# Self attention: a select on GpSimd in place of the second causal mask on TensorE

## The chip, the cores and the metric

The kernel runs on one NeuronCore of a Trainium2 chip. The metric is the device time of one execution in microseconds (us). Matrix products run on TensorE (PE in the profile), reductions out of PSUM and norms on VectorE (DVE), exponentials and most copies out of PSUM on ScalarE (ACT), small elementwise work and gather or scatter DMAs on GpSimd (POOL).

## The reference, cut to what matters

Four blocks work on 32 batches of 112 rows with 256 columns: cross attention to a context, causal self attention, a mixture of eight experts, and a second cross attention with a quantised layer. The change lies in the second:

```
nx = layernorm(x, ln1_w, ln1_b)
q, k, v = split(nx @ Wqkv + bqkv, 3)             # 16 heads of 16
scores = einsum('bqhd,bkhd->bhqk', q, k) / sqrt(16)
scores = where(tril(ones), scores, finfo.min)    # a query sees no later key
attn = softmax(scores)
x = x + einsum('bhqk,bkhd->bqhd', attn, v).reshape(B, S, D) @ Wo + bo
```

A layernorm, the choice of two experts for each row, and the scatter of the rows to the experts' slots follow in the same loop.

## The kernel before, in words

`program` (L1734 on) calls four stages one after another: `cross_first`, `self_attention`, `experts`, `cross_last`. Each keeps one instruction stream per engine, and the streams meet only in semaphores. An engine works through its own stream in order: a wait holds back all that is written behind it. Those streams, written by hand, set the order of the work; nothing else plans it.

`self_attention` goes over the 32 batches with `over_batches`, whose function `step(b, par)` is called for b from -2 to 35. One step works on up to seven batches in different phases. For the batch b:

- TensorE, in this order within step b: `plain_scores` of b (four matmuls that write the mask `causal` at L1019, then 16 of q by k at L1028) into the four banks of `quad`; `values` of b-1 (16 matmuls at L1051, from `probsT` into `outs`); the expert logits and the rank of earlier batches (L1083, L258); q of b+1 (L1060); transposes of the attention's output of b-1 into rows (L1096); k of b+1 (L1060); transpose of the maxima of b (L1103); transposes of the normalised rows of b-1 (L1107); `scores` of b; transposes for b-2 (L1119); the output product of b-1 (L1125); v of b+1 (L1130); transposes of b+2 (L1137).
- `scores` writes the scores of b a second time into `quad`, transposed, with the keys on the partitions. The mask `causal_t` comes first (four matmuls of 448 columns, L1019), then the negated row maxima (16, L1036), then k by q (8, L1041). ScalarE takes exp of all 1792 columns into `probsT` (L864); `probsT` lies in a part of the tensor that the trace names `w`. Its sums come from a column of ones in `v`, inside `values`.
- VectorE in step b: statistics of b+2 (L231, L234), maxima of b out of `plain_scores` (L938), rank, reciprocal and product of b-1 (L951, L953), norm of b+2, norm of b-2, `place` and `choose` for older batches, norm of b+2 into `nn` (L245), then the output of b-1: L976, L979, its statistics, and v of b+1 (L986).
- GpSimd in step b: rstd of b+2 (L238, L240) and two instructions that keep it (L796, L797); q times the mask of heads (L801); rstd (L238, L240); two scatters of b-4 (L812); the residual of b-1 (L817), which waits for `o_added` from L979; rstd (L238, L240); a copy of b-2 (L824).

`held` instructions of one element (L810, L823) stand between a wait and the instruction that it is for. Two waits of TensorE's stream matter below: ahead of `plain_scores`, `wait(pe, exp_ready, b)`, since it overwrites `quad`; ahead of `values`,

```
pe.wait_ge(exp_ready, b)
pe.wait_ge(v_ready, b)
wait(pe, o_biased, b - 1)
values(1 - par)
```

Of the kernel before, what the change touches and what calls it, by code (L numbers as in the profile page):

```python
# [16 lines left out]
ALU = mybir.AluOpType  # L17
# [4 lines left out]
T = 112  # L22
# [18 lines left out]
def wait(eng, sem, value):  # L41

    if isinstance(value, int) and value <= 0:
        return
    eng.wait_ge(sem, value)


def exists(b, n=NB):

    return not isinstance(b, int) or 0 <= b < n  # L50


def over_batches(eng, step, before=1, after=1, first=2, last=2):


    for b in range(-before, first):
        step(b, b % 2)
    with eng.Fori(first // 2, (NB - last) // 2) as i:
        step(2 * i, 0)
        step(2 * i + 1, 1)  # L60
    for b in range(NB - last, NB + after):
        step(b, b % 2)
# [199 lines left out]
def row(ap, b):  # L262

    return ap[0:T, bass.ds(b, 1), :].rearrange("p a d -> p (a d)")
# [425 lines left out]
def self_attention(nc, mem, w, residual):  # L690
# [3 lines left out]
    with ExitStack() as ctx:  # L694
        sb = lambda n, shape, dt=F32: ctx.enter_context(nc.sbuf_tensor(f"s_{n}", shape, dt))
        sem = lambda n: ctx.enter_context(nc.semaphore(f"s_{n}"))
# [5 lines left out]
        ident_bf, causal, causal_t = (sb(n, [T, T], BF16) for n in ("ident_bf", "causal", "causal_t"))  # L702
        late = mem["w2"][:, NE - 1, :, :].rearrange("p c d -> p (c d)")
        probsT = late[0:T, 0:16 * T].rearrange("p (r c) -> p r c", r=4)
# [39 lines left out]
        scores_mm, exp_ready, values_mm = sem("scores_mm"), sem("exp_ready"), sem("values_mm")  # L744
        oT_ready, rows_mm, recip_ready, on_ready = sem("oT_ready"), sem("rows_mm"), sem("recip_ready"), sem("on_ready")
        oT2_mm, oT2_ready, op_mm, o_biased, o_added = sem("oT2_mm"), sem("oT2_ready"), sem("op_mm"), sem("o_biased"), sem("o_added")
        x_ready, stats_kept, n2_kept = sem("x_ready"), sem("stats_kept"), sem("n2_kept")
        n2T_mm, n2T_ready, gate_mm, gate_ready = sem("n2T_mm"), sem("n2T_ready"), sem("gate_mm"), sem("gate_ready")
        choose_step, chosen_ready, rank_mm, place_step, slot_ready = (sem(n) for n in ("choose_step", "chosen_ready", "rank_mm", "place_step", "slot_ready"))
# [18 lines left out]
        with nc.Block() as block:  # L768

            @block.sync  # L770
            def _(sp):
                sp.sem_clear(mem["spent"])
                for dst, src in loads:
                    sp.dma_start(dst, src).then_inc(weights_in, 16)
                for t in range(2):
                    for e in range(2):
                        for r in range(4):
                            at = (8 * t + 2 * r + e) * HD
                            sp.dma_start(wo[64 * e + HD * r:64 * e + HD * (r + 1), t, :], w["L0_ffn_Wo"][at:at + HD, :]).then_inc(wo_in, 16)
                sp.dma_start(mem["fc1_b"][:, :, :], w["L0_ffn_fc1_b"]).then_inc(mem["fc1_b_in"], 16)  # L780
                for e in range(NE - 1):
                    sp.dma_start(mem["w2"][:, e, :, :], w["fc2_t"][e].rearrange("(c p) d -> p c d", p=128)).then_inc(mem["w2_in"], 16)
                sp.wait_ge(values_mm, NB)
                sp.dma_start(mem["w2"][:, NE - 1, :, :], w["fc2_t"][NE - 1].rearrange("(c p) d -> p c d", p=128)).then_inc(mem["w2_in"], 16)

            @block.gpsimd
            def _(pool):
                pool.wait_ge(cleared, 1)
                pool.wait_ge(mem["slots_cleared"], 32 * (NB - 2))

                def step(b, par):
                    nxt, ahead = b + 1, b + 2
                    if exists(ahead):
                        norm_u.pool_rstd(pool, ahead)
                        pool.wait_ge(norm_u.rstd_ready, 2 * ahead + 2)
                        pool.tensor_copy(row(u_stats, ahead)[:, 0:1], norm_u.rstd[:, 1:2])  # L796
                        pool.tensor_tensor(row(u_stats, ahead)[:, 1:2], norm_u.moments[:, 0:1], norm_u.rstd[:, 1:2], ALU.mult)\  # L797
                            .then_inc(stats_kept, 1)
                    if exists(nxt):
                        pool.wait_ge(q_whole, nxt + 1)  # L800
                        pool.tensor_tensor(qT[1 - par][:, :, :, :], q[:, :, :].unsqueeze(2).to_broadcast([128, 2, 2, T]),  # L801
                                           mem["qmask"][:, :].unsqueeze(1).unsqueeze(3).to_broadcast([128, 2, 2, T]), ALU.mult)\
                            .then_inc(q_ready, 1)
                    if exists(ahead):
                        norm_n.pool_rstd(pool, ahead)
                    if exists(b - 4):
                        pool.wait_ge(slot_ready, b - 3)
                        pool.wait_ge(n2_kept, b - 3)

                        pool.tensor_tensor(held[:, 2 + par:3 + par], mem["minus_half"][0:1, :], mem["minus_half"][0:1, :], ALU.add)  # L810
                        for i in range(TOP):
                            pool.indirect_dma_start(mem["slots"], bass.IndirectOffsetOnAxis(ap=slot_now[par][i][:, :], axis=0),  # L812
                                                    n2_sent[par][:, :], None).then_inc(sent[par], 16)
                    if exists(b - 1):
                        pool.wait_ge(o_added, b)
                        x = row(residual, b - 1)
                        pool.tensor_tensor(x, x, y_rows[1 - par][:, :], ALU.add).then_inc(x_ready, 1)  # L817
                        norm_o.pool_rstd(pool, b - 1)
                    if exists(b - 2):
                        pool.wait_ge(norm_o.rows_ready, b - 1)  # L820
                        wait(pool, sent[par], 16 * (b - par - 2))

                        pool.tensor_tensor(held[:, par:par + 1], mem["minus_half"][0:1, :], mem["minus_half"][0:1, :], ALU.add)  # L823
                        pool.tensor_copy(n2_sent[par][:, :], n2[:, :]).then_inc(n2_kept, 1)  # L824

                over_batches(pool, step, 2, 4, 4)
                for i in range(2):
                    pool.wait_ge(sent[i], 16 * TOP * NB // 2)
# [180 lines left out]
            def _(pe):  # L1009
# [3 lines left out]
                def step(b, par):  # L1013
# [3 lines left out]
                    def masked(mask):  # L1017
                        for r in range(4):
                            pe.matmul(quad[0:T, r, 0:4 * T].rearrange("p (h t) -> p h t", h=4), ident_bf[:, :],  # L1019
                                      mask[:, :].unsqueeze(1).to_broadcast([T, 4, T]), start=True, stop=False, skip_group_check=True)  # L1020
# [9 lines left out]
                        last.then_inc(plain_mm, 1)  # L1030

                    def scores():
                        masked(causal_t)
                        for h in range(4):
                            for r in range(4):
                                pe.matmul(quad[0:T, r, h * T:(h + 1) * T], choice[group(r), h, :], shift[group(r), :],  # L1036
                                          start=False, stop=False, skip_group_check=True)
                        for t in range(2):
                            for r in range(4):
                                at = 2 * t * T  # L1040
                                last = pe.matmul(quad[0:T, r, at:at + 2 * T], kT[par][group(r), t, :],  # L1041
                                                 qT[par][group(r), t, :, :].rearrange("p e t -> p (e t)"),
                                                 start=False, stop=True, skip_group_check=True)
                        last.then_inc(scores_mm, 1)
# [28 lines left out]
                        wait(pe, exp_ready, b)  # L1073
                        plain_scores()
                    if exists(b - 1):
                        pe.wait_ge(exp_ready, b)
                        pe.wait_ge(v_ready, b)
                        wait(pe, o_biased, b - 1)
                        values(1 - par)
# [29 lines left out]
                    if exists(b):  # L1109
                        pe.wait_ge(shift_ready, b + 1)  # L1110
                        scores()
# [20 lines left out]
                    if exists(ahead):  # L1132
# [5 lines left out]
                        last.then_inc(nT_mm, 1)  # L1138

                over_batches(pe, step, 2, 4, 4)  # L1140
                pe.wait_ge(slot_ready, NB)
                pe.matmul(rank_out, ones[:, :], earlier[:, :], start=True, stop=True).then_inc(total_mm, 1)
# [660 lines left out]
```

## Time and profile before

| what | value |
|---|---|
| median of 3 runs | 2145.3 us (2142.04 to 2145.58) |
| the profiled execution, its own time | 2148.3 us |
| its span, first to last instruction | 2146.3 us |
| TensorE busy | 1999.6 us (93%) |
| VectorE busy | 1390.0 us (65%) |
| ScalarE busy | 1022.8 us (48%) |
| GpSimd busy | 889.4 us (41%) |
| mean granted TensorE clock | 0.971 of full speed |

The self attention takes the stretch from about 537 to 902 us of the span. The busy share of the whole says little of one stage, so what is read is one step of its loop, engine by engine. A time in front of a row is its start from the beginning of the span; "idle before" is how long the engine had nothing to do, and `<-` names what ended it.

### The profile page before, as it was taken

The numbers are of one execution on the slowest core, as the hardware profiler recorded it, in microseconds if no ns is written. First come the engines' busy times: TensorE is split into PE (matmuls) and PEld (weight loads), VectorE is DVE, ScalarE is ACT, GpSimd is POOL, SyncE is SP. The second block draws the span as 40 slices with busy tenths as digits, with TensorE's granted clock in tenths as the row PEclk, the third lists the DMA queues.
The fourth block names the chain that finished last, engine by engine and source line by source line (L and its number), as shares of the span: only waits on it lengthen the run. The fifth ranks groups of instructions, "written<-read, shape, count | busy, mean of one in ns | idle before, by whom it ended". The sixth has DMA issues, their size and how long they took to land. (4 is left out here: it accounts for less than half of the span.)

```text
span 2146.3 us, 61038 instructions
## 1 busy us (share of the span) xinstructions
PE 1999.6 (93%) x21235; PEld 1659.7 (77%) x21236; DVE 1390.0 (65%) x3586; ACT 1022.8 (48%) x2370; POOL 889.4 (41%) x1479
## 2 busy tenths in 40 slices
PE   5999999996899999589999999779999999999996
PEld 4888888885677777479999999657777777777774
DVE  5777777773688888543333333247887878788875
ACT  2555555553444444223223232246666666666662
POOL 4454554541466666400000000145656666665651
PEclk9999999998999999799999999979999999999998
DMA  7223323251400000111111111210111111011100
GB/s 209 90 85 103 95 92 105 82 210 29 143 22 21 21 21 21 51 57 37 34 39 34 37 37 34 87 34 22 37 31 36 31 29 39 27 39 29 36 20 9
DMA packets 98810, 118.87 MB, mean 55 GB/s; under 512 B 9794, under 2 KB 91458, under 8 KB 98626
## 3 DMA queue, kind: packets, MB, share of 16 engines
q1 hardware_dynamic: 92610, 103.43, 15.8%
q0 software_dynamic: 6144, 14.69, 2.3%
q8 instruction: 36, 0.59, 0.1%
q14 instruction: 20, 0.16, 0.0%
HBM read 67.36 MB, written 50.72 MB: 55 GB/s over the span
## 5 line engine op out<-in xcount | busy, mean ns | idle before, releaser
L1245 ACT ACTIVATE e_act_T<-ps_quad,fc_b 128x128 f32<-128x128 f32 x504 | 136.8, 383 | 313.3 <-PE ps_quad L1310 313.3
L1310 PEld LDWEIGHTS ps_quad<-e_xT,e_w_now 128*128 128x128 f32 x2016 | 236.4, 193 | 7.9 <-DVE e_xT L1279 4.1
L1310 PE MATMUL ps_quad<-e_xT,e_w_now 128*128 128x128 f32 x2016 | 237.4, 276 | 3.5 <-DVE e_xT L1279 3.5
L1325 PE MATMUL ps_out<-w,e_act_T 128*128 x1008 | 228.1, 379 | 0.8 <-DVE e_y L1287 0.8
L1423 POOL COPY c_index<-slot 112x1 uint32 (+1 forms) x64 | 19.4, 332 | 477.7 <-POOLq L1208 477.7
L419 ACT ACTIVATE a_probsT<-ps_quad 125x1792 f32<-125x1792 f32 x96 | 159.9, 1665 | 100.6 <-PE ps_quad L579 100.6
L1276 DVE COPY e_w_now<-w 128x2048 f32 x63 | 77.3, 1227 | 200.2 <-PE ps_quad L1310 190.3
L1325 PEld LDWEIGHTS ps_out<-w,e_act_T 128*128 128x128 f32 x1008 | 186.6, 190 | 24.0 <-issue 1.2
L1450 POOL TENSOR_TENSOR c_kL<-c_kT,c_kH 128x376 fp32r<-128x376 f32 x128 | 126.3, 986 | 172.0 <-ACT c_kH L1502 171.4
L206 ACT ACTIVATE c_probs<-ps_quad,c_negmax 112x375 f32<-112x375 f32 x256 | 144.0, 571 | 29.7 <-DVE c_negmax L167 29.7
L1497 ACT ACTIVATE c_kT<-ps_proj 128x376 f32<-128x376 f32 x128 | 61.9, 484 | 182.8 <-PE ps_proj L258 181.4
L167 DVE TENSOR_REDUCE c_negmax<-ps_quad 112x2 f32<-112x750 f32 x128 | 120.0, 937 | 43.4 <-PE ps_quad L136 35.2
L178 DVE TENSOR_SCALAR c_probs<-c_probs,c_recip 112x375 f32<-112x375 f32 x256 | 144.0, 603 | 4.6
L476 DVE TENSOR_REDUCE a_negmax<-ps_turned 112x2 f32<-112x750 f32 x128 | 120.2, 939 | 33.8 <-PE ps_turned L565 33.7
L474 DVE TENSOR_REDUCE a_negmax<-ps_quad 112x4 f32<-112x1500 f32 x64 | 110.2, 1722 | 36.6 <-PE ps_quad L565 36.6
L258 PE MATMUL ps_proj<-c_cH,c_wkH 128*128 128x376 f32 x256 | 100.3, 392 | 32.3 <-DVE c_wvH L1564 20.8
L147 PE MATMUL ps_turned<-ident,c_probs 112*125 112x112 f32 x768 | 107.9, 277 | 1.6 <-DVE c_probs L178 1.4
L147 PEld LDWEIGHTS ps_turned<-ident,c_probs 112*125 112x125 f32 x768 | 96.3, 189 | 10.4 <-issue 10.0
L1287 DVE TENSOR_TENSOR e_y<-ps_out,e_b 128x256 f32<-128x256 f32 x63 | 26.7, 424 | 119.0 <-PE ps_out L1325 119.0
L158 PE MATMUL ps_out<-c_probsT,c_v 125*64 125x112 f32 x1536 | 101.9, 268 | 0.2 <-ACT c_probsT L199 0.2
L158 PEld LDWEIGHTS ps_out<-c_probsT,c_v 125*64 125x64 f32 x1536 | 74.5, 136 | 34.6 <-issue 30.5
L199 ACT ACTIVATE c_probsT<-ps_turned 125x672 f32<-125x672 f32 x128 | 93.8, 733 | 4.7 <-PE ps_turned L147 4.7
(308 smaller groups left out, 5331.6 us busy)
## 6 DMA issues: line engine op xcount, KB each, us to landing
slots<-a_zeros SPq DMA_DIRECT2D x60, 512.0 KB, 4.9
a_cT<-in_ctx_t SPq DMA_DIRECT2D x32, 375.0 KB, 3.6
c_cT<-in_ctx_t SPq DMA_DIRECT2D x32, 375.0 KB, 3.2
w<-in_fc_t SPq DMA_DIRECT2D x2, 4096.0 KB, 20.1
w<-in_fc_t SPq DMA_DIRECT2D x8, 1024.0 KB, 11.7
e_xg<-slots SPq DMA_DIRECT2D x63, 128.0 KB, 2.0
slots<-e_y SPq DMA_DIRECT2D x63, 128.0 KB, 1.7
out<-c_fo SPq DMA_DIRECT2D x32, 112.0 KB, 1.9
```

What stands on the lines that cost most here:

```text
L147: last = pe.transpose(self.turned[u % sets][:, j, c * T:(c + 1) * T], self.probs[u % 4][:, j, c * self.chunk:(c + 1) * self.chunk], ident[ ...
L158: last = pe.matmul(self.out[row:row + self.vdim, block * T:(block + 1) * T], v(u, j, c), self.probsT[u % 2][:, j, c, :], start=(c == 0), s ...
L167: dve.tensor_reduce(self.negmax[:, u % 4, :], self.scores[u % len(self.scores)], AX, ALU.max, negate=True).then_inc(self.max_ready, 1)
L178: last = dve.tensor_scalar(p, p, self.recip[:, u % 4, j:j + 1], None, ALU.mult)
L206: last = act.activation(self.probs[u % 4][:, j, :], self.scores[u % len(self.scores)][:, j, :], ACT.Exp, bias=self.negmax[:, u % 4, j:j + ...
L419: act.activation(probsT[:, 2 * i:2 * i + 2, :, :].rearrange("p c r x -> p r c x"), quad[0:KC, :, 0:2 * HALF].rearrange("p r (c x) -> p r c ...
L474: dve.tensor_reduce(rows[:, :, 0], quad[0:T, :, 0:CTX], AX, ALU.max, negate=True).then_inc(max_ready, 1)
L476: dve.tensor_reduce(rows[:, 2 * half:2 * half + 2, 0], plain[0:T, :, 0:CTX], AX, ALU.max, negate=True)\
L1245: last = act.activation(act_T[par][:, c * TILE:(c + 1) * TILE], hidden[par][:, c // 4, (c % 4) * TILE:(c % 4 + 1) * TILE], ACT.Gelu, bias= ...
L1310: last = pe.matmul(hidden[par][:, c // 4, (c % 4) * TILE:(c % 4 + 1) * TILE], w1_now[:, k, c * 128:(c + 1) * 128], xT[par][:, k, :], start ...
L1325: last = pe.matmul(y_ps[:, 0:D], act_T[1 - par][:, c * TILE:(c + 1) * TILE], w2[:, bass.ds(e, 1), c, :].rearrange("p a d -> p (a d)"), sta ...
L1450: pool.tensor_tensor(kL[to][:, tile, :], kT[:, tile, :], kH[to][:, tile, :], ALU.subtract).then_inc(k_ready, 1)
```

## The change

GpSimd gets a new piece in step b, behind its first norm and ahead of the product with the mask of heads. It waits until the exponentials of batch b-1 are there, and sets to zero, in place, all those of `probsT` whose key (partition) is later than its query (column). TensorE writes no `causal_t` into `quad`; the first matmul of each group now starts the sum. `values` waits for `causal_ready` from GpSimd in place of `exp_ready`. The mask of `plain_scores` stays, so the row maxima are still taken over the allowed keys alone.

```diff
+        causal_ready, mask_held = sem("causal_ready"), sb("mask_held", [1, 1])
...
                         pool.tensor_tensor(row(u_stats, ahead)[:, 1:2], norm_u.moments[:, 0:1], norm_u.rstd[:, 1:2], ALU.mult)\
                             .then_inc(stats_kept, 1)
+                    if exists(b - 1):
+                        pool.wait_ge(exp_ready, b)
+                        pool.tensor_tensor(mask_held[:, :], mem["minus_half"][0:1, :], mem["minus_half"][0:1, :], ALU.add)
+                        pool.affine_select(probsT, probsT, [[0, 4], [0, 4], [1, T]], ALU.is_ge, 0.0, base=0, channel_multiplier=-1).then_inc(causal_ready, 1)
                     if exists(nxt):
                         pool.wait_ge(q_whole, nxt + 1)
...
                     def scores():
-                        masked(causal_t)
                         for h in range(4):
                             for r in range(4):
                                 pe.matmul(quad[0:T, r, h * T:(h + 1) * T], choice[group(r), h, :], shift[group(r), :],
-                                          start=False, stop=False, skip_group_check=True)
+                                          start=True, stop=False, skip_group_check=True)
...
                     if exists(b - 1):
-                        pe.wait_ge(exp_ready, b)
+                        pe.wait_ge(causal_ready, b)
                         pe.wait_ge(v_ready, b)
                         wait(pe, o_biased, b - 1)
                         values(1 - par)
```

How the instructions of GpSimd follow one another in the loop's step, before (a row names the output, then the inputs; ISA and REGISTER_ALU are waits and counters):

```order
L796 COPY s_u_stats<-s_norm_u_rstd 112x1
L797 ISA
L797 TENSOR_TENSOR s_u_stats<-s_norm_u_moments,s_norm_u_rstd 112x1
L801 TENSOR_TENSOR s_qT<-s_q,qmask 128x448
L238 TENSOR_TENSOR s_norm_n_rstd<-s_norm_n_moments,eps 112x1
```

And after:

```order
L797 COPY s_u_stats<-s_norm_u_rstd 112x1
L798 ISA
L798 TENSOR_TENSOR s_u_stats<-s_norm_u_moments,s_norm_u_rstd 112x1
L802 TENSOR_TENSOR s_mask_held<-minus_half 1x1
L803 AFFINE_SELECT w<-w 112x1792
L806 TENSOR_TENSOR s_qT<-s_q,qmask 128x448
L238 TENSOR_TENSOR s_norm_n_rstd<-s_norm_n_moments,eps 112x1
```

The select stands last behind everything that GpSimd does for the step before and behind the rstd of b+2; the product for q of b+1 stands behind it.

TensorE in the loop's step, before, from the transposes of b-1 to the `values` of the next step:

```order
L1107 MATMUL ps_out<-ident,s_on 128x112 x2
L1019 MATMUL ps_quad<-s_causal_t,s_ident_bf 112x448 x4
L1036 MATMUL ps_quad<-s_shift,s_choice 112x112 x16
L1041 MATMUL ps_quad<-s_qT,s_kT 112x224 x8
L1119 MATMUL ps_turned<-ident,s_n 128x112 x2
L1125 MATMUL ps_out<-s_wo,s_oT 112x256 x2
L1130 MATMUL ps_turned<-s_wqkv,s_nT 112x256 x2
```

And after:

```order
L1111 MATMUL ps_out<-ident,s_on 128x112 x2
L1040 MATMUL ps_quad<-s_shift,s_choice 112x112 x16
L1045 MATMUL ps_quad<-s_qT,s_kT 112x224 x8
L1123 MATMUL ps_turned<-ident,s_n 128x112 x2
L1129 MATMUL ps_out<-s_wo,s_oT 112x256 x2
L1134 MATMUL ps_turned<-s_wqkv,s_nT 112x256 x2
```

Four mask matmuls are gone; all else keeps its place, `values` included.

## Rows read from the trace of the kernel before

**Rows 1.** Page, busy times; then PE, PEld, DVE, ACT, POOL, clock, steady stretch.

```profile
PE 1999.6 (93%) x21235; PEld 1659.7 (77%) x21236; DVE 1390.0 (65%) x3586; ACT 1022.8 (48%) x2370; POOL 889.4 (41%) x1479
...
600.00:860.00 260.00, 257.01 (x3566) 205.35 (x3566) 219.45 (x908) 126.94 (x295) 168.02 (x374) 1.00 0.07 22
```

**Rows 2.** Timeline of TensorE, one step: start us, us, what, [idle before].

```profile
620.19 1.05 PE L1028 MATMUL ps_quad<-s_kT,s_qT 32*112 32x112 f32 x32
621.17 0.97 PE L1051 MATMUL ps_out<-w,s_v 112*32 112x112 f32 x32
...
623.56 0.60 PE L1096 MATMUL ps_out<-ident,s_oT 128*112 128x128 f32 x4
...
624.97 0.41 PE L1107 MATMUL ps_out<-ident,s_on 112*128 112x112 f32 x2
625.49 0.96 PE L1019 MATMUL ps_quad<-s_causal_t,s_ident_bf 112*112 112x448 bf16 x4
...
627.97 1.03 PE L1125 MATMUL ps_out<-s_wo,s_oT 128*112 128x256 f32 x4
...
629.70 0.36 PE L1137 MATMUL ps_proj<-ident,s_nn 112*128 112x112 f32 x2
...
631.73 0.97 PE L1051 MATMUL ps_out<-w,s_v 112*32 112x112 f32 x32
```

**Rows 3.** Timelines: two exponentials on ScalarE, the matmul after the first.

```profile
554.73 1.66 ACT L864 ACTIVATE w<-ps_quad 112x1792 f32<-112x1792 f32 x1 [1.95 <-PE ps_quad L1041]
...
556.53 0.94 PE L1019 MATMUL ps_quad<-s_causal,s_ident_bf 112*112 112x448 bf16 x4 [0.65 <-ACT w L864]
...
627.87 1.67 ACT L864 ACTIVATE w<-ps_quad 112x1792 f32<-112x1792 f32 x1 [1.70 <-PE ps_quad L1041]
```

**Rows 4.** Timeline of VectorE in the same step.

```profile
624.20 0.26 DVE L951 RECIPROCAL s_recip<-ps_out 112x16 f32<-112x16 f32 x1 [0.61 <-PE ps_out L1096]
...
628.72 0.41 DVE L245 TENSOR_SCALAR s_nn<-s_u_rows,s_norm_n_moments,s_norm_n_rstd 112x256 f32<-112x256 f32 x1
629.16 0.48 DVE L976 SCALAR_TENSOR_TENSOR s_o<-ps_out,s_u_stats,s_bo 112x256 f32<-112x256 f32 x1
```

**Rows 5.** Timeline of GpSimd in the same step and the one before.

```profile
623.27 0.19 POOL L797 TENSOR_TENSOR s_u_stats<-s_norm_u_moments,s_norm_u_rstd 112x1 f32 x1
...
630.52 0.72 POOL L817 TENSOR_TENSOR residual<-residual,s_y_rows 112x256 f32 x1 [0.42 <-issue]
...
632.01 0.18 POOL L823 TENSOR_TENSOR s_held<-minus_half 1x1 f32<-1x1 f32 x1
632.14 0.39 POOL L824 COPY s_n_sent<-s_n 112x256 f32<-112x256 f32 x1
...
633.63 0.19 POOL L797 TENSOR_TENSOR s_u_stats<-s_norm_u_moments,s_norm_u_rstd 112x1 f32 x1
```

**Rows 6.** Groups of GpSimd instructions: count, busy us, mean ns, idle before.

```profile
L377 POOL TENSOR_TENSOR a_cL<-a_cT,a_cH 128x376 fp32r<-128x376 f32 x64 | 62.2, 993 | 2.6
...
L801 POOL TENSOR_TENSOR s_qT<-s_q,qmask 128x448 f32<-128x448 f32 x32 | 29.8, 932 | 41.3 <-ACT s_q L845 41.3
L371 POOL CAST a_cH<-a_cT 128x376 fp32r<-128x376 f32 x64 | 29.8, 489 | 0.0
```

**Rows 7.** Stretches of 2 us, columns as in rows 1, around idle TensorE.

```profile
882.00:884.00 2.00, 0.60 (x3) 0.18 (x1) 0.82 (x2) 0.96 (x1) 0.55 (x1) 1.00 0.29 90
920.00:922.00 2.00, 2.00 (x13) 2.00 (x13) 0.00 (x0) 0.00 (x0) 0.00 (x0) 0.58 0.11 36
...
1436.00:1438.00 2.00, 1.48 (x9) 1.20 (x10) 0.62 (x1) 0.00 (x0) 2.00 (x3) 0.77 0.00 0
```

**Rows 8.** Timeline of TensorE, other stretches: an idle time and two speeds.

```profile
889.02 2.02 PE L1125 MATMUL ps_out<-s_wo,s_oT 128*112 128x256 f32 x4 [0.17 <-ACT s_oT L860]
...
918.01 5.57 PE L1310 MATMUL ps_quad<-e_xT,e_w_now 128*128 128x128 f32 x32 [0.82 <-DVE e_xT L1279]
...
1436.52 0.43 PE L136 MATMUL ps_quad<-c_kH,c_qH 64*112 64x376 f32 x2 [1.78 <-issue]
```

## The prediction

> **What bounds the kernel now.** I read the page first: TensorE is busy for 1999.6 us, 93% of the span [rows 1]. Then the stretch from 600 to 860 us, in the middle of the self attention: TensorE is busy for 257.0 of 260 us at full clock, VectorE for 219, GpSimd for 168 [rows 1]. So TensorE sets the pace there, and a first reading says that four matmuls less per batch are a pure gain. A gain on a full engine only counts if nothing new is put into its path, so the timeline of one step comes next. The `values` matmuls start at 621.17 and those of the next step at 631.73, so a step takes about 10.55 us [rows 2], and no row of TensorE between them shows an idle time.
>
> The question is where the new wait of `values` ends. The exponentials are not the issue: they run from 627.87 to 629.54 [rows 3], two microseconds ahead of `values` at 631.73. The select however stands in GpSimd's stream behind L797, and L797 of the step whose `values` start at 621.17 begins at 623.27 and ends at 623.46 [rows 5]. GpSimd comes to the select 2.3 us after TensorE wants its result. That is the core of the case: the wait is late by GpSimd's place in line, before the select has cost anything.
>
> **A ring that closes.** A late wait would be paid once if GpSimd did not depend on it. It does. I follow the ring from one `values` to the next, each piece from the start of one row to the start of the next:
>
> - `values` 621.17 to VectorE's reciprocal at 624.20: 3.03 us, in which TensorE does `values`, logits, rank, q and the transposes L1096 (end 624.16) [rows 2, 4].
> - reciprocal 624.20 to L976 at 629.16: 4.96 us. L976 needs the output product L1125 (627.97, end 629.00) [rows 2], but VectorE itself ends `nn` (L245) at 629.13 [rows 4]. VectorE's own queue sets this piece.
> - L976 to GpSimd's residual L817 at 630.52: 1.36 us [rows 4, 5].
> - L817 to the end of L797 at 633.63 + 0.19 = 633.82: 3.30 us of GpSimd's stream in one piece [rows 5].
>
> Sum: 12.65 us, against a step of 10.55. Today nobody waits for that end, so it costs nothing. Behind the change `values` waits for it.
>
> **The change part by part.**
>
> - Removed, four mask matmuls per batch: the `causal_t` block at 625.49 takes 0.96 us [rows 2]; its last matmul runs beside the next block, so I count 0.9 us of TensorE per step, 29 us for 32 batches. In the ring it saves nothing: L1125 would end at 628.1 in place of 629.00, and L976 still waits for VectorE at 629.13. I take 0; the ends are 0 and 0.1.
> - Added, one `mask_held`: as L823 to L824, 632.01 to 632.14, it moves the stream by 0.13 us [rows 5].
> - Added, the wait from GpSimd to TensorE: the nearest row is exp to mask, end 556.39, start 556.53 [rows 3]: 0.14 us.
> - Added, the select itself, 112 partitions by 1792 elements. The trace has no such instruction. From below: one input, 376 elements in 489 ns [rows 6]; with 0.19 us for an instruction of one element (L797) [rows 5] that is 0.80 ns for each further element, so 0.19 us + 1791 x 0.80 ns = 1.62 us. From above: two inputs, 376 elements in 993 ns, 2.14 ns each, 4.02 us. The product of L801, with two inputs of which one is repeated, takes 932 ns for 448 [rows 6], or 1.66 ns each: 3.2 us. The select reads one input but must make up a second value and compare, so it lies between the copy and L801. I take 2.8 us and keep 1.62 and 4.02.
>
> The Trainium skill, GPSIMD Engine Reference, section "Performance pitfalls for Q7 kernels", gives bodies that compare and select 2.03 cycles for an element, or 1.03 when unrolled by two, at the 1.2 GHz of its section "Specifications". As an estimate that is 3.0 or 1.5 us here, and the step would be 0.2 us longer or 1.3 us shorter than mine; no row of this trace shows a select.
>
> Step with TensorE at full clock: 12.65 + 0.13 + 2.8 + 0.14 = 15.72 us, that is 5.17 longer.
>
> - The clock. In that step TensorE has work up to the end of `plain_scores`. They end at 621.2 today, 10.55 us behind the `values` before. Without the masks they could end 0.9 sooner, but L1137 waits for `nn` (629.13 against 629.70 today [rows 2, 4]), so the saving is 0.5 and they end 10.1 us behind `values`. Until 15.7 TensorE stands still, 5.6 us in each step. What a gap can do is in the trace: an idle time of only 1.78 us ahead of 1436.52 lies in a stretch whose mean clock fell to 0.77 [rows 7, 8], so it dropped to the lower level in it. Against it stands 882 to 884, with TensorE busy for 0.60 of 2 us and the clock at 1.00 [rows 7]. With 5.6 us I expect the drop to 1.2 GHz in nearly each step. It ends only after TensorE has worked again for a while: the matmuls that began at 918.01 behind an idle time were still slow for most of 920 to 922, mean 0.58 [rows 7, 8], so some 3.7 us. At the low clock a block takes twice as long: L1125 2.02 us at 889.02, against 1.03 [rows 2, 8]. The first piece of the ring, 2.99 us of TensorE work, is what falls into that. With 3.7 us slow it grows by 1.85, if slow throughout by 2.99. I take 2.4. The piece from reciprocal to L976 stays VectorE's as long as the clock is back by then.
>
> A step: 15.72 + 2.4 = 18.1 us, 7.57 longer. There are 32 `values`, so 31 intervals: 235 us. The first and last steps have less of GpSimd's work and more of other waits, which I leave at zero. The profiled execution took 2148.3 us, so 2383; the median of the runs lies 3 below it: **2380 us**.
>
> **What is late next, and who queues.** Behind the select on GpSimd stands L801, the product for q of the next batch. It needs a product that TensorE starts only behind `values`, and idles 41.3 us in 32 times for it today [rows 6], so it loses nothing. The scatters follow and the residual, which already waits for L979. `plain_scores` of the next batch and VectorE's maxima run while TensorE waits for the select.
>
> **The rivals.**
>
> 1. *The ring, but the clock holds.* For it: 882 to 884. Against it: 1436 [rows 7]. Then 31 x 5.17 = 160 us more: 2305. With a select of 1.62 or 4.02 us it is 2268 or 2343. Chance 0.20.
> 2. *The clock stays low past the transposes.* Then the first piece grows by 2.99, and TensorE's work from L1107 at 624.97 to the end of L1125 at 629.00 [rows 2], 4.0 - 0.9 = 3.1 us without the masks, takes 6.3 against the 4.2 in which VectorE gets to L976 and adds 2.1. A step is 15.72 + 2.99 + 2.1 = 20.8 us, 10.3 longer: 2145 + 318 = 2463. For it: TensorE has short waits in that piece too, which could keep the clock down. Against it: work without a pause had the clock back after 3.7 us at 918. Chance 0.10.
> 3. *Faster: the select is hidden.* If GpSimd reached the select early enough, behind the exponentials' end at 629.54 and done by 631.73, the 29 us come in whole: 2116. It would need GpSimd to be through with L797 by 631.73 - 2.8 - 0.3 = 628.6, and today that is 633.82. L817 alone, which waits for `o_added`, keeps it beyond that. The point from which it decides is the select's start against `values`; the rows have it 5 us on the wrong side. Chance 0.02.
> 4. *The change does not take its price*: the select costs so little or the ring bends so that the step stays at 10.6 us. Nothing in the rows supports it. Chance 0.01.
>
> The forecast has 0.67. Its own range, by the select's ends (-37 and +38 us) and the clock's (-17 and +18), is 2326 to 2436. The range from 2280 to 2450 takes in most of rival 1 and leaves out most of rival 2. A measurement of this kernel tells 0.2%, some 4 us, from no change. Only rival 3 is faster, only rival 4 is the same, all the rest is slower by far.
>
> **What would show it.** In the profile after: GpSimd's select starts right behind `mask_held`, with a mean time between 1.62 and 4.02 us; TensorE has 32 idle times ahead of the `values` matmuls, ended by the select, some 5 us each; between two starts of `values` lie 17 to 19 us; VectorE's piece from reciprocal to L976 is still near 5 us; the granted clock in the middle of the stage is well under 1.00, about 0.8, and `values` at the head of each step take about twice 0.97 us. The other three stages keep their times. It is wrong if the stage's TensorE rows show no idle time there, or if the step is longer than 20 us with a select under 4.

## The result, and the profile after

| what | before | after |
|---|---|---|
| median, measured side by side | 2144.97 us (4 runs) | 2334.69 us (4 runs, 2332.72 to 2337.71) |
| the profiled execution, its own time | 2148.3 us | 2337.7 us |
| its span | 2146.3 us | 2335.9 us |
| mean granted TensorE clock | 0.971 | 0.918 |

The ratio of the medians is 1.0889 (the 95% interval is 1.087 to 1.0908), so the change costs 190 us. The forecast was 2380, its range 2280 to 2450. In the profile after, the lines of the self attention have moved by four or five: the select is L803, `values` L1055, the reciprocal L956, L976 is now L981, L979 is L984, L1125 is L1129, L817 is L822.

The page's busy times after:

```profile
PE 2072.1 (89%) x21107; PEld 1739.8 (74%) x21108; DVE 1388.6 (59%) x3586; ACT 1022.9 (44%) x2370; POOL 951.0 (41%) x1543
```

The same stretch of 600 to 860 us as in [rows 1], with the columns told there:

```profile
600.00:860.00 260.00, 195.47 (x2143) 167.12 (x2135) 132.75 (x559) 77.31 (x180) 133.96 (x264) 0.75 0.04 13
```

TensorE has 128 matmul records less than before, and yet it is busy for 72 us more. In the stretch it is busy for 195 us where it was 257, at a mean clock of 0.75 where it was 1.00. Fewer matmuls, more busy time and a lower clock belong together: each matmul at the low clock is counted for longer. Every engine has idle time in the stretch, so no engine bounds it. That is what a ring of waits looks like.

The group of the select after (busy us, mean ns, idle before):

```profile
L803 POOL TENSOR_SCALAR_AFFINE_SELECT w<-w 112x1792 f32<-112x1792 f32 x32 | 57.4, 1793 | 0.0
```

And the view of waits in the stage (us in total, times, longest):

```profile
PE ps_out L1055 <- POOL w L803: 124.7, 32, 5.1
```

The select takes 1.79 us, not the 2.8 of the prediction. All 32 `values` wait for it, 3.9 us each. Now the timeline of TensorE over one step after, to be laid beside [rows 2]:

```profile
655.99 1.72 PE L1055 MATMUL ps_out<-w,s_v 112*32 112x112 f32 x32 [4.17 <-POOL w L803]
...
660.42 1.06 PE L1100 MATMUL ps_out<-ident,s_oT 128*112 128x128 f32 x4
...
665.35 1.03 PE L1129 MATMUL ps_out<-s_wo,s_oT 128*112 128x256 f32 x4
...
668.12 1.05 PE L1033 MATMUL ps_quad<-s_kT,s_qT 32*112 32x112 f32 x32
673.22 0.97 PE L1055 MATMUL ps_out<-w,s_v 112*32 112x112 f32 x32 [4.04 <-POOL w L803]
```

The same step on VectorE and GpSimd, to be laid beside [rows 4, 5]:

```profile
661.51 0.26 DVE L956 RECIPROCAL s_recip<-ps_out 112x16 f32<-112x16 f32 x1 [2.43 <-PE ps_out L1100]
...
666.54 0.48 DVE L981 SCALAR_TENSOR_TENSOR s_o<-ps_out,s_u_stats,s_bo 112x256 f32<-112x256 f32 x1 [0.37 <-PE ps_out L1129]
...
667.89 0.72 POOL L822 TENSOR_TENSOR residual<-residual,s_y_rows 112x256 f32 x1 [0.75 <-DVE s_y_rows L984]
671.00 0.19 POOL L798 TENSOR_TENSOR s_u_stats<-s_norm_u_moments,s_norm_u_rstd 112x1 f32 x1
671.15 0.18 POOL L802 TENSOR_TENSOR s_mask_held<-minus_half 1x1 f32<-1x1 f32 x1
671.29 1.79 POOL L803 TENSOR_SCALAR_AFFINE_SELECT w<-w 112x1792 f32<-112x1792 f32 x1
```

The ring can be walked in these rows from 655.99 to 673.22: `values` to reciprocal 5.52 us (predicted 3.03 plus 2.4 of clock), reciprocal to L981 5.03 (4.96), L981 to the residual 1.35 (1.36), the residual to the end of L798 3.30 (3.30), `mask_held` and select to `values` 2.03. In the step after it the same ring loses its time elsewhere:

```profile
678.00 0.26 DVE L956 RECIPROCAL s_recip<-ps_out 112x16 f32<-112x16 f32 x1 [2.50 <-PE ps_out L1100]
...
683.49 0.48 DVE L981 SCALAR_TENSOR_TENSOR s_o<-ps_out,s_u_stats,s_bo 112x256 f32<-112x256 f32 x1 [0.81 <-PE ps_out L1129]
...
690.10 1.72 PE L1055 MATMUL ps_out<-w,s_v 112*32 112x112 f32 x32 [4.17 <-POOL w L803]
```

Here `values` to reciprocal is 4.78 us, and reciprocal to L981 5.49, because VectorE waits 0.81 us for the output product. Steps of 17.25 us, like the first, and of 16.88, like the second, follow one another, 17.07 on average. The first three and the last three of the 31 are shorter: 12.1, 15.4, 16.2, and 15.9, 12.0, 14.6.

The clock in slices of 1 us (the column behind the five engines):

```profile
653.00:654.00 1.00, 0.00 (x0) 0.00 (x0) 1.00 (x1) 0.00 (x0) 0.84 (x3) 0.81 0.00 0
654.00:655.00 1.00, 0.00 (x0) 0.00 (x0) 0.02 (x1) 0.00 (x0) 1.00 (x3) 0.50 0.00 0
...
663.00:664.00 1.00, 1.00 (x12) 0.67 (x14) 0.85 (x6) 0.62 (x3) 0.60 (x2) 0.57 0.00 0
664.00:665.00 1.00, 1.00 (x32) 0.78 (x28) 0.68 (x8) 0.38 (x2) 0.47 (x3) 1.00 0.00 0
...
674.00:675.00 1.00, 1.00 (x14) 0.88 (x6) 0.00 (x0) 0.54 (x1) 0.00 (x0) 0.55 0.00 0
```

The clock falls from 2.4 to 1.2 GHz in the idle time and comes back near 663.9, after 7.9 us of work without a pause. In the next step `values` still run at full clock (673.22, 0.97 us); the clock falls 0.9 us after they began, and the matmuls behind them are slow all the same. The idle time had ended by then. The low clock of this step lasts from 674.1 to about 680.9, 6.8 us. A slow stretch need not start inside the gap ahead of it. The trace of before shows the same behind the idle time that ended at 1436.52 [rows 8]: in slices of 1 us the clock is 1.00 up to 1437 and 0.55 in the next.

The signs that the prediction named came in the main: 32 idle times ended by the select, a select between 1.62 and 4.02 us, steps of 17.07 us in the middle, at the lower end of 17 to 19, and a clock of 0.75 there. The idle times are 3.9 us where some 5 were expected, and `values` take twice 0.97 us in every second step only.

### The profile page after: what moved, and what is told of

It is laid out like the page before. It is cut to its first block and busy times, and to the rows that moved or that the text cites. A ratio compares the mean times of both kernels' runs of the same rounds, so it can differ in the third digit from the quotient of the medians.

```text
span 2335.9 us, 60849 instructions
## 1 busy us (share of the span) xinstructions
PE 2072.1 (89%) x21107; PEld 1739.8 (74%) x21108; DVE 1388.6 (59%) x3586; ACT 1022.9 (44%) x2370; POOL 951.0 (41%) x1543
## 3 DMA queue, kind: packets, MB, share of 16 engines
q1 hardware_dynamic: 92610, 103.43, 14.4%
## 5 line engine op out<-in xcount | busy, mean ns | idle before, releaser
L1055 PE MATMUL ps_out<-w,s_v 112*32 112x112 f32 x1024 | 43.6, 330 | 124.7 <-POOL w L803 124.7
L178 DVE TENSOR_SCALAR c_probs<-c_probs,c_recip 112x375 f32<-112x375 f32 x256 | 148.9, 622 | 4.6
L1055 PEld LDWEIGHTS ps_out<-w,s_v 112*32 112x32 f32 x1024 | 33.1, 139 | 130.9 <-POOL w L803 76.4
L845 ACT ACTIVATE s_oT<-ps_out 128x448 f32<-128x448 f32 x32 | 17.4, 544 | 200.6 <-PE ps_out L1055 200.6
```

Source lines behind the costliest of these rows:

```text
L178: last = dve.tensor_scalar(p, p, self.recip[:, u % 4, j:j + 1], None, ALU.mult)
```

## The experiments

Ten kernels ran. Each edit is shown against the kernel after; a "step" is the distance between the starts of two `values`. Each ratio is to the kernel before, measured beside it: 2149.63 us for the first four, 2150.89 for the sixteen products and for the select behind the residual, 2148.68 for the other four. The kernel after was measured once, beside 2144.97, so its difference to these ten is good to some 6 us.

**The wait alone.** Is it the select's duration or GpSimd's place in line that costs?

```diff
-pool.tensor_tensor(mask_held[:, :], ..., ALU.add)
-pool.affine_select(probsT, ...).then_inc(causal_ready, 1)
+pool.tensor_tensor(mask_held[:, :], ..., ALU.add).then_inc(causal_ready, 1)
...
 def scores():
+    masked(causal_t)
```

> The select is left out and the causal_t mask of TensorE is back, so the arithmetic is that of the kernel before; what stays of the change is the place of the wait: values waits for the one-element instruction on GpSimd behind L797. Ring theory: the step is 12.65 + 0.13 + 0.14 = 12.9 us with the clock held, 31 x 2.4 us more than before, so 2145 + 73 = 2218 us; if the shorter idle time of TensorE (some 2.3 us a step) still costs clock, up to 1.85 us a step more, 2276 us. Rival, the select's own time is the cost and the place is harmless: 2145 us, within 5.

Measured: 2268.67 us, ratio 1.0552 (1.0533 to 1.057). With no select, and with TensorE's mask as before, the wait costs 119 us. Two starts of `values` from TensorE's timeline:

```profile
654.87 0.97 PE L1055 MATMUL ps_out<-w,s_v 112*32 112x112 f32 x32 [2.08 <-POOL s_mask_held L802]
...
667.91 1.56 PE L1055 MATMUL ps_out<-w,s_v 112*32 112x112 f32 x32 [2.41 <-POOL s_mask_held L802]
```

That step is 13.04 us long, near the ring's 12.65 plus one small instruction. Others take up to 16.8, and the mean is 14.4: an idle time of some 2 us is already followed by the low clock in many steps (mean 0.89 between 600 and 860 us). So the place in line costs before any select has run; the view that the price is the select's alone, and this kernel as fast as the one before, falls.

**The mask left out.** What are the four matmuls worth by themselves? The select is out, `values` waits for `exp_ready`, and TensorE writes no `causal_t`, so this kernel doesn't mask later keys in the exponentials.

```diff
-if exists(b - 1): ... pool.affine_select(probsT, ...)
...
-pe.wait_ge(causal_ready, b)
+pe.wait_ge(exp_ready, b)
```

> The causal_t mask is left out and nothing put in its place (later keys are not masked in the exponentials); values waits for exp_ready as before. Theory: outside the ring the four matmuls are worth their 0.9 us a step, 29 us in all: 2116 us; if VectorE or GpSimd bound the shorter step first, 2120 to 2130. Rival, the masks are hidden beside other work anyway: 2145 us.

Measured: 2132.42 us, ratio 0.9923 (0.99 to 0.9946), 17 us less. That is over half of the 29 us that TensorE's rows promise. The stretch from 600 to 860 us shows both engines, TensorE at 248 of 260 us where it was 257, and VectorE at 221 where it was 219 [rows 1]:

```profile
600.00:860.00 260.00, 248.20 (x3535) 196.56 (x3534) 221.28 (x927) 133.13 (x303) 170.51 (x372) 1.00 0.07 23
```

TensorE's timeline says why no more is won:

```profile
653.72 0.41 PE L1137 MATMUL ps_proj<-ident,s_nn 112*128 112x112 f32 x2 [0.33 <-DVE s_nn L245]
```

TensorE now waits for `nn` in each of the 25 steps between 600 and 860 us, 7.0 us in all: VectorE is next in line. The prediction had it so and let 0.5 of the 0.9 us through; in the middle it is 0.22, steps of 10.33 us for 10.55. The shorter steps at both ends give the rest, and a first `values` that comes 3.3 us sooner. So the most that this change could have brought with VectorE's stream as it is, is some 17 us.

**The select ahead of the residual**, in the same step as its exponentials.

```diff
-if exists(b - 1): pool.wait_ge(exp_ready, b) ...            # behind L798
+if exists(b): pool.wait_ge(exp_ready, b + 1) ...            # behind the scatters
```

> The same select, moved in GpSimd's stream from behind L797 of the next step to ahead of the residual (L817 of the kernel before), behind the two scatters. Ring theory: it starts when the scatters end, 8.9 us behind values, and ends at 10.8, so the step is about 11.0 us: 2150 to 2180 us. Rival, GpSimd's extra 1.8 us a step is what costs, wherever it stands: it stays near 2335 us.

Measured: 2174.23 us, ratio 1.0116 (1.0097 to 1.0135). The same instructions, put elsewhere in GpSimd's stream, cost 25 us in place of 190. The clock in the middle stays at 1.00 and the steps are 11.6 us long. Part of what is left has a cause that I had not expected. The group of L984 on VectorE:

```profile
L984 DVE SCALAR_TENSOR_TENSOR s_y_rows<-residual,s_u_stats,s_o 112x256 f32<-112x256 f32 x32 | 74.3, 2321 | 4.9 <-DVE s_o L981 4.7
```

And one of its rows in the timeline beside the select on GpSimd:

```profile
643.08 2.60 DVE L984 SCALAR_TENSOR_TENSOR s_y_rows<-residual,s_u_stats,s_o 112x256 f32<-112x256 f32 x1 [0.18 <-DVE s_o L981]
...
643.60 1.79 POOL L818 TENSOR_SCALAR_AFFINE_SELECT w<-w 112x1792 f32<-112x1792 f32 x1
```

L984 took 0.485 us before and takes 2.32 us now. It ends at 645.68, just behind the select's end at 645.39. That adds 1.8 us per step to VectorE, the engine that is next in line. The next reciprocal starts 3.8 or 4.1 us behind `values`, where it was 3.0. The step is 0.6 us longer than the ring's 11.0; how much of the 25 us is this hold and how much the ring, is not measured apart.

**The select ahead of the scatters**, earlier still.

```diff
-if exists(b - 1): pool.wait_ge(exp_ready, b) ...            # behind L798
+if exists(b): pool.wait_ge(exp_ready, b + 1) ...            # ahead of the scatters
```

> The same select, moved further up, ahead of the two scatters. It can start when the exponentials are there, 7.4 us behind values, and ends at 9.4, ahead of the 9.7 us that TensorE needs for a step without the masks. Ring theory: 9.7 to 10.6 us a step, 2118 to 2147 us; GpSimd then has some 9.7 us of work and gaps per step and may bound it itself. Rival, GpSimd's extra time is what costs wherever it stands: near 2335 us.

Measured: 2219.17 us, ratio 1.0325 (1.0306 to 1.0344): a clear miss. Between 600 and 860 us no wait of `values` for the select is left. The group of `nn` on VectorE:

```profile
L245 DVE TENSOR_SCALAR s_nn<-s_u_rows,s_norm_n_moments,s_norm_n_rstd 112x256 f32<-112x256 f32 x32 | 45.9, 1434 | 7.2 <-POOL s_norm_n_rstd L240 7.2
```

And a row of TensorE's timeline that waits for it:

```profile
714.49 0.41 PE L1141 MATMUL ps_proj<-ident,s_nn 112*128 112x112 f32 x2 [1.89 <-DVE s_nn L245]
```

Here the select stands beside `nn`, which takes 1.43 us in place of 0.41, up to 2.1. TensorE waits 1.9 us for it, and the clock falls in many steps (mean 0.89 between 600 and 860 us, steps of 12.6 to 13.8 us). In the four of the 20 steps in which `nn` runs free, another is held: L984 twice, and twice L913, a product of 112x16 (1.81 us in place of 0.17). The wait was gone and the contention had taken its place. How the 70 us divide between the hold and the clock is not measured.

**The gap filled, too long.** If the low clock is a cost of its own, matmuls without use in the gap should give it back.

```diff
+wait(pe, o_biased, b - 1)
+for i in range(30):
+    pe.matmul(outs[:, 0:128], ident[:, :], ident[:, :], ...)
 pe.wait_ge(causal_ready, b)
 pe.wait_ge(v_ready, b)
-wait(pe, o_biased, b - 1)
```

> The changed kernel with 30 more matmuls of TensorE (identity by identity, 128 columns, into the bank that values overwrites) behind plain_scores and ahead of the wait for the select. They compute nothing that is used; they fill some 3.5 of the 4.2 us in which TensorE stands idle. Clock theory: of the 6 us that a step is longer, 4.2 are the ring with the clock held and 1.85 the lower clock behind the gap; with the gap filled the granted clock stays near 1.00, the step is 12.65 + 0.13 + 1.79 + 0.14 = 14.7 us and the kernel takes about 2145 + 129 = 2275 us. Rival, the clock is only a symptom and the ring does not run over TensorE's slow part: 2335 us or more.

Measured: 2354.99 us, ratio 1.0955 (1.0937 to 1.0973). The filling was sized wrongly. Thirty such products took twice the time that I had given them, and themselves held `values` back by 2.9 us behind the select's end at 644.04:

```profile
640.06 6.96 PE L1082 MATMUL ps_out<-ident 128*128 128x128 f32 x60
646.95 0.97 PE L1055 MATMUL ps_out<-w,s_v 112*32 112x112 f32 x32
```

The clock did stay at 1.00, but the time said nothing. So it was repeated with about half as many.

**The gap filled, short enough.** The same edit with `range(16)`.

> The kernel after, with 16 matmuls of the identity with itself (128 columns) ahead of the wait of `values` for the select; their result in `outs` is overwritten by `values`. Thirty of them took 6.96 us, 0.23 us each, so 16 take 3.7 us, and the gap that they fill, from the end of `plain_scores` (10.1 us behind `values`) to the select's end (14.6), is 4.5 us at full clock: they end before the select. Theory (the ring is 12.65 + 0.13 + 1.79 + some 0.1 = 14.7 us, and the rest of what the change costs is the lower clock of the steps' beginnings): step 14.7 us, clock near 1.00, in all 2149 + 31 x 4.15 = 2278 us, 57 us faster than the kernel after. Rival (the rest is not the clock but other waits of the ring, which an idle TensorE does not cause): no gain, 2335 us, with steps of 16.5 us at whatever clock.

Measured: 2268.50 us, ratio 1.055 (1.0533 to 1.0568). Sixteen useless products per batch make the kernel after 66 us faster. The middle of the stage:

```profile
600.00:860.00 260.00, 244.54 (x3099) 204.63 (x3101) 159.04 (x663) 94.75 (x216) 155.27 (x300) 1.00 0.05 16
```

TensorE, VectorE and GpSimd in one step:

```profile
645.99 0.97 PE L1055 MATMUL ps_out<-w,s_v 112*32 112x112 f32 x32 [0.58 <-POOL w L803]
...
656.42 3.84 PE L1082 MATMUL ps_out<-ident 128*128 128x128 f32 x32
660.47 0.97 PE L1055 MATMUL ps_out<-w,s_v 112*32 112x112 f32 x32 [0.21 <-POOL w L803]
...
649.01 0.26 DVE L956 RECIPROCAL s_recip<-ps_out 112x16 f32<-112x16 f32 x1 [1.11 <-PE ps_out L1102]
...
653.87 0.48 DVE L981 SCALAR_TENSOR_TENSOR s_o<-ps_out,s_u_stats,s_bo 112x256 f32<-112x256 f32 x1
...
655.22 0.72 POOL L822 TENSOR_TENSOR residual<-residual,s_y_rows 112x256 f32 x1 [0.29 <-issue]
...
658.49 0.18 POOL L802 TENSOR_TENSOR s_mask_held<-minus_half 1x1 f32<-1x1 f32 x1
```

This is the ring at full clock: 3.02, 4.86, 1.35 and 3.27 us up to `mask_held`, then 0.14, 1.79 and 0.05 to `values` at 660.47, 14.48 in all. Steps of 14.49 and 14.63 alternate, 14.56 on average. The steady steps of the kernel after are 17.07, so the clock costs 2.51 us in each. In the first of the two steps shown for the kernel after it lies in the first piece, 5.52 against 3.02. In the second, 1.76 lie there (4.78) and 0.5 or 0.6 in the piece to L981 (5.49 against 4.86 here and 4.99 in the steps between), which waits for a late output product. Here L981 does not wait for it.

**The mask back on TensorE**, with the select kept. The prediction gave the removed matmuls nothing.

```diff
 def scores():
+    masked(causal_t)
```

> The changed kernel with the causal_t mask of TensorE written again, beside the select. The prediction has the removed mask at nothing, since VectorE's own queue holds L976: 2335 us. The profile after shows L981 (L976 before) waiting 0.74 us a step for the output product, because TensorE was slow ahead of it, so part of the 0.9 us should come back: 2335 + 20 to 28 = 2355 to 2363 us.

Measured: 2366.45 us, ratio 1.1013 (1.0995 to 1.1032), 32 us above the kernel after. Within the profiled executions the mean step goes from 16.56 to 17.33 us, 24 us in all, so I put it at 24 to 32. Some steps take 17.1 us, as without the masks, others up to 18.7. VectorE's row shows where a late step loses:

```profile
652.82 0.48 DVE L981 SCALAR_TENSOR_TENSOR s_o<-ps_out,s_u_stats,s_bo 112x256 f32<-112x256 f32 x1 [1.84 <-PE ps_out L1130]
```

In the kernel after L981 waited 0.4 or 0.8 us for the output product; in the late steps here it waits 1.5 to 1.9, so the masks push that product back by about a microsecond, and it is in the ring.

**The select twice** on the same data, the second behind its own wait and `mask_held`.

```diff
-pool.affine_select(probsT, ...).then_inc(causal_ready, 1)
+pool.affine_select(probsT, ...).then_inc(first_done, 1)
+pool.wait_ge(first_done, b)
+pool.tensor_tensor(mask_held[:, :], ..., ALU.add)
+pool.affine_select(probsT, ...).then_inc(causal_ready, 1)
```

> The changed kernel with the select executed twice, one behind the other with a semaphore and a one-element instruction between. Ring theory: every microsecond of GpSimd ahead of causal_ready is a microsecond of each of 31 steps, so 1.79 + 0.15 to 0.3 us each, 60 to 65 us: 2395 to 2400 us; if the longer idle time of TensorE costs more clock, up to 1.1 us a step on top, 2434 us. Rival, the select's time is partly hidden: under 2365 us.

Measured: 2442.40 us, ratio 1.1366 (1.1347 to 1.1385), 108 us more, or 3.5 per step. The two selects start 2.02 us apart:

```profile
647.92 1.79 POOL L804 TENSOR_SCALAR_AFFINE_SELECT w<-w 112x1792 f32<-112x1792 f32 x1
...
649.94 1.79 POOL L807 TENSOR_SCALAR_AFFINE_SELECT w<-w 112x1792 f32<-112x1792 f32 x1
651.87 1.72 PE L1059 MATMUL ps_out<-w,s_v 112*32 112x112 f32 x32 [6.04 <-POOL w L807]
```

So 2.0 us of the 3.5 is the ring, one for one, and the rest came with more time at the low clock (mean of the span 0.904 against 0.918). Its greater part stands in the piece from the reciprocal to L985 (L981 of the kernel after), which takes 5.7 and 7.0 us in turn in most of the middle, where it took 5.03 and 5.49:

```profile
724.52 0.48 DVE L985 SCALAR_TENSOR_TENSOR s_o<-ps_out,s_u_stats,s_bo 112x256 f32<-112x256 f32 x1 [2.44 <-PE ps_out L1133]
```

The first piece is 5.52 us in every step now. This is what rival 2 of the prediction describes, the clock low past the transposes. The time lies 8 us above the highest that was expected of the run.

**The select in quarters**, at the place ahead of the residual: if a VectorE instruction is held only until the running GpSimd instruction ends, four short ones should hold it less.

```diff
+for r in range(4):
+    part = pool.affine_select(probsT[:, r, :], ..., [[0, 4], [1, T]], ...)
+part.then_inc(causal_ready, 1)
```

> The select ahead of the residual as in the run before_residual, cut into four selects of 448 columns. There VectorE's L984, with both inputs in SBUF, took 2.3 us in place of 0.48 beside the select. Port theory: it waits until the instruction running on GpSimd ends, so with quarters of some 0.5 us L984 takes at most 1.0 us, VectorE gains 1.3 us a step and the kernel takes 2150 to 2165 us, against 2174. Rival, it waits for the whole piece of GpSimd work or for something else: L984 stays at 2.3 us and the time at 2174 or a little over.

Measured: 2184.32 us, ratio 1.0158 (1.0141 to 1.0175), 10 us slower than the single select at that place. The two groups, and the rows of two steps:

```profile
L986 DVE SCALAR_TENSOR_TENSOR s_y_rows<-residual,s_u_stats,s_o 112x256 f32<-112x256 f32 x32 | 29.0, 907 | 4.9 <-DVE s_o L983 4.0 <-issue 0.7
...
L819 POOL TENSOR_SCALAR_AFFINE_SELECT w<-w 112x448 f32<-112x448 f32 x128 | 70.1, 574 | 0.0
...
634.14 2.18 POOL L819 TENSOR_SCALAR_AFFINE_SELECT w<-w 112x448 f32<-112x448 f32 x4
634.46 2.14 DVE L986 SCALAR_TENSOR_TENSOR s_y_rows<-residual,s_u_stats,s_o 112x256 f32<-112x256 f32 x1 [0.18 <-issue]
...
645.82 0.67 DVE L986 SCALAR_TENSOR_TENSOR s_y_rows<-residual,s_u_stats,s_o 112x256 f32<-112x256 f32 x1 [0.18 <-DVE s_o L983]
646.20 0.34 POOL L817 TENSOR_TENSOR s_mask_held<-minus_half 1x1 f32<-1x1 f32 x1
646.50 2.18 POOL L819 TENSOR_SCALAR_AFFINE_SELECT w<-w 112x448 f32<-112x448 f32 x4
```

VectorE's instruction falls from 2.32 to 0.91 us on average, but not as the theory had it. In most steps, as at 645.82, L986 now goes first: GpSimd's `mask_held` takes 0.34 us in place of 0.18, and the quarters start when L986 has ended. Six times in the profiled execution L986 started as the first quarter began or ran. Five times, as at 634.46, it took 2.14 to 2.48 us and ended 0.28 us behind the last quarter, so it was not let in between them; once it was, behind the first (0.59 us). That speaks for the rival, the whole piece of GpSimd's work, and against a hold that ends with the instruction. Why L986 comes first here in steps in which it did not beside the single select, the runs do not show.

The time is a miss too. Four selects take 2.18 us from first start to last end against 1.79, L986 pushes them back where it goes first, `values` wait 34.4 us for them in total where they waited 19.7, and the clock falls in some steps: those of 11.58 us, much as before, are mixed with others of 12.0 to 12.6.

**The select behind the residual**, a place that the ring prices by itself, and where VectorE reads PSUM beside it.

```diff
 pool.tensor_tensor(x, x, y_rows[1 - par][:, :], ALU.add).then_inc(x_ready, 1)
+if exists(b): pool.wait_ge(exp_ready, b + 1) ... pool.affine_select(...)
 norm_o.pool_rstd(pool, b - 1)
```

> The select of batch b stands in step b right behind the residual of b-1 and ahead of the norm that follows it. Theory (the ring alone sets it): `values` to the residual 3.03 + 4.96 + 1.36 = 9.35 us, the residual 0.72, one small instruction 0.13, the select 1.79, to TensorE 0.1: a step of 12.1 us, 1.55 longer than before, 2149 + 48 = 2197 us with the clock held. The idle time that TensorE then has ahead of `values` is some 2.0 us; in the run with the wait alone about as much cost 1.5 us per step through the clock, and with that it is 2243. Rival (what costs is only the contention of the select with VectorE's instructions, which here stands at another place, beside the copy of the last q, k or v and the statistics): under 2180 us.

Measured: 2212.93 us, ratio 1.0267 (1.0227 to 1.0306), with single runs from 2198 to 2228. From its timelines:

```profile
647.35 0.72 POOL L818 TENSOR_TENSOR residual<-residual,s_y_rows 112x256 f32 x1 [0.34 <-issue]
648.04 0.18 POOL L821 TENSOR_TENSOR s_mask_held<-minus_half 1x1 f32<-1x1 f32 x1
648.06 0.42 DVE L231 BATCH_NORM_STATS2 s_norm_u_stats<-residual 112x6 f32 x1
648.18 1.79 POOL L822 TENSOR_SCALAR_AFFINE_SELECT w<-w 112x1792 f32<-112x1792 f32 x1
...
648.62 2.00 DVE L944 TENSOR_REDUCE s_negmax<-ps_quad 112x16 f32<-112x1792 f32 x1
...
650.03 1.17 PE L1056 MATMUL ps_out<-w,s_v 112*32 112x112 f32 x32 [1.77 <-POOL w L822]
```

Steps at full clock take 12.04 us; the ring gave 12.1. Others take 13.4 to 15.4, with the clock low in part of them. The mean clock of the four runs, 0.951 to 0.965, goes with their times, the lowest with the longest. The rival (contention alone, under 2180) falls: L985 is back at 485 ns, and the maxima L944, read from PSUM beside the select, take their 2.0 us as ever. So do the statistics L231, which read the residual in SBUF, with 0.42 us.

None of the four placements of the select beats the kernel before. Only the kernel without the mask does, and it leaves out part of the computation.

## Why the prediction was right, and where its sizes were off

- **The ring** (12.65 us at full clock) held. With the clock held it measures 12.50 us up to `mask_held`, and each piece agrees within 0.1. The other placement was priced from the same rows at 12.1 and came out at 12.04. Moving the select takes away up to 165 of the 190 us, and the wait alone, without a select, costs 119, so the place in GpSimd's stream decides.
- **The select** was priced at 2.8 us between 1.62 and 4.02, and takes 1.79. This term failed most: 1.01 us x 31 = 31 us too much. I argued that a compare must lie above a copy. The group of the select [after, above] puts its elements at (1.79 - 0.19) / 1791 = 0.89 ns, near the 0.80 of the copy in [rows 6] and far from the 1.66 and 2.14 of the products. That fits a price by the number of inputs read, but these are four kinds of work and no run varied the inputs alone. The estimate from the Trainium skill, GPSIMD Engine Reference, section "Performance pitfalls for Q7 kernels", was 3.0 or 1.5 us; the trace sides with the faster of its two figures, and with neither exactly.
- **The joints.** With a select of 1.79 my terms give 14.71 us at full clock, and 14.56 are measured: `mask_held` began before L798 had ended, and the handover to TensorE took 0.05 or 0.06 us where I had 0.14. That is 0.15 us x 31 = 4.7 us.
- **The clock** at 2.4 us per step measures 2.51, and that agreement is partly luck. I had slow work last 3.7 us, from the stretch at 918 to 922 [rows 7, 8]; here it lasts 7.9 and 6.8 us in turn. I had all of the cost in the first piece, which grows by 2.5 us in one kind of step and by 1.76 in the other, 2.13 on average. The rest is the start of rival 2: L981 waits 0.4 or 0.8 us for the output product (23.8 us in 32 steps), and its piece takes 5.03 or 5.49 us against 4.86 or 4.99 with the gap filled. "VectorE's own queue sets this piece" therefore holds at full clock and fails in the kernel after: there L981 waits for TensorE's output product in every step between 600 and 860 us.
- **The removed masks** were priced at 0. At full clock that is nearly so: L981 has no wait for the output product with the gap filled, and its piece takes 4.86 or 4.99 us without the masks, 4.96 with them in the kernel before and 5.16 with them in the wait alone (a step of 13.04 us). In the slowed ring they are worth 24 to 32 us, as the run with the mask back shows. The zero did not spoil the sum, since I put nothing on that piece for the clock either, and without the masks it stays at 5.03 and 5.49 us; the sentence that they save nothing in the ring was wrong.
- **The first and last steps** I left at the length of the others. Over the first three and last three, the kernel after is 16 us short of 6 x 17.07, the kernel before 1.5 short of 6 x 10.55. That is 14.6 us.

Together these give 31 + 4.7 + 14.6 = 50 us too much, less 31 x 0.11 = 3.4 for the clock, so some 47 us, and the forecast lay 45 above the result. Filling the gap leaves 118 us above the kernel before measured beside it: that is the ring at full clock. Of the cost of 190 us the clock is then 66 to 72 us (2334.69 against 2268.50, or 190 less 118; the kernel before stood 6 us higher in that comparison). Rival 1 is the 118 us: its 2305, with 31 us less for the select, is 2274. Its price of the ring was right, and that the clock holds by itself was not.

## What to carry to other kernels

Before a wait is moved to another engine, follow that engine's stream to the point at which it gets there, and ask whether its arrival depends on the consumer's last step. If it does, the lateness isn't paid once but in every step, whatever the new instruction costs. Then look at what runs beside the new place: ahead of the scatters TensorE was free of the wait, but VectorE was held and the clock fell, and the kernel took 2219 us where the place behind the scatters took 2174. A removed instruction is worth what the engine that comes next in line lets through, 17 of 29 us here.

## What the runs showed that I had not expected

- **Some VectorE instructions are held by GpSimd's work, and some hold it.** Beside the select, L984, which reads two tensors in SBUF, takes 2.32 us instead of 0.485, and `nn` 1.43 instead of 0.41 (1.9 to 2.1 where it is held). Both end just behind the select. Not all are held: the maxima out of PSUM (2.00 us) and the statistics L231 out of SBUF (0.42 us) are as long as ever beside it. Four selects without a pause mostly held L986 as one does. The order of the starts does not decide alone: the row of L984 at 643.08 starts 0.5 us ahead of the select and ends behind it. In the other direction, a `mask_held` that came while L986 ran took 0.34 us in place of 0.18. The hint stood in the trace of before: VectorE's other L245, which writes `u_rows` beside GpSimd's L801, takes 727 ns there on average. In the kernel after it takes 404, since it starts only when that product (now L806) is about to end. I had read past it.
- **Small idle times cost the clock irregularly.** With 2 us idle ahead of `values` some steps run at full clock and the next ones don't (12.04 and 15.4 us in one kernel), and the time varies by 1.3% from run to run, where all the others stay within 0.4%. What decides between the two is not shown.
- **Useless work can pay.** Sixteen products of 0.24 us that fill 3.84 us of a gap of about 4 gave back 66 us; thirty, which overran it, lost 20. The kernel before is still faster than either.
